# Second attention of a four-layer kernel: a pair's output product is issued before a head's products and transposed banks on TensorE

## What is computed

```python
q = jnp.einsum('qdh,bcd->bhcq', Q, x) * sq
k = jnp.einsum('qdh,bcd->bhcq', K, x) * sq
v = jnp.einsum('vdh,bcd->bhcv', V, x) * sv
att = jnp.einsum('bhcq,bhCq->bhcC', q, k) / d_query
att = jnp.where(causal, att, -jnp.inf)
p = jax.nn.softmax(att, axis=-1)
y = jnp.einsum('bhcC,bhCv->bhcv', p, v)
z = jnp.einsum('dvh,bhcv->bcd', W, y) * (math.sqrt(d_embed / d_value) / num_heads)
```

## Time and profile before

| | |
|---|---|
| median of 3 runs | 1491.33 us (1491.08 to 1492.69) |
| the profiled execution | 1491.82 us, span 1490.1 us |
| PE, busy of the span | 1212.1 us (81%) |
| DVE | 1099.0 us (74%) |
| ACT | 946.7 us (64%) |
| POOL | 757.9 us (51%) |

### The profile page before, as it was taken

One profiled execution on the slowest core, in us unless ns is written; L12 is line 12 of the kernel. 1 busy time (PEld: TensorE's weight loads), 2 busy tenths in 40 slices (PEclk: granted clock), 3 DMA queues, 4 the chain that ended last, 5 costly groups with the idle time before them and its releaser, 6 DMA issues. The chain is left out here.

```text
span 1490.1 us, 28115 instructions
## 1 busy us (share of the span) xinstructions
PE 1212.1 (81%) x7865; PEld 1037.6 (70%) x7865; DVE 1099.0 (74%) x2826; ACT 946.7 (64%) x2522; POOL 757.9 (51%) x950
## 2 busy tenths in 40 slices
PE   1587734999928898988998999999999997299992
PEld 1476633999817777777777777777777776199992
DVE  5666534777727788888888888888888886277774
ACT  1554421444418788888888888889898886154440
POOL 3004463444405555576575576675765765334443
PEclk9986656999959999999999999999999998599996
DMA  9391011222125656555555556565555652122215
GB/s 182 102 379 61 29 38 45 62 60 61 40 71 128 142 128 140 130 133 139 125 129 136 127 136 141 131 153 128 135 135 127 139 131 47 31 63 60 61 52 175
DMA packets 122658, 165.15 MB, mean 111 GB/s; under 512 B 40164, under 2 KB 84079, under 8 KB 122512
## 3 DMA queue, kind: packets, MB, share of 16 engines
q1 hardware_dynamic: 109648, 144.34, 41.1%
q0 software_dynamic: 8640, 16.93, 3.6%
q10 hardware_dynamic: 4224, 2.10, 0.5%
HBM read 26.59 MB, written 36.96 MB: 43 GB/s over the span
## 5 line engine op out<-in xcount | busy, mean ns | idle before, releaser
L1389 POOL TENSOR_TENSOR b_probs<-b_probs,b_recip 128x128 f32<-128x128 f32 (+3 forms) x512 | 352.1, 717 | 294.8 <-DVE b_recip L1622 294.8
L420 DVE TENSOR_TENSOR b_pt_lo<-b_ring,b_pt_hi 128x512 fp32r<-128x512 f32 (+1 forms) x384 | 229.7, 598 | 104.1 <-ACT b_pt_hi L414 101.7
L545 ACT ACTIVATE b_probs<-b_s_bank,b_neg_max 128x256 f32<-128x256 f32 (+3 forms) x512 | 266.2, 530 | 47.9 <-DVE b_neg_max L537 47.9
L1227 POOL DMA_INDIRECT y_rows<-f_y_sb,f_dest x142 | 138.8, 978 | 193.0 <-DVE f_y_sb L1200 185.2
L537 DVE TENSOR_REDUCE b_neg_max<-b_s_bank 128x1 f32<-128x256 f32 (+3 forms) x512 | 219.2, 479 | 11.1 <-PE b_s_bank L529 10.9
L1437 PE MATMUL b_s_bank<-b_stack 128*128 128x256 f32 (+3 forms) x1024 | 208.0, 338 | 13.8 <-DMA b_stack<-b_qk 7.5
L414 ACT ACTIVATE b_pt_hi<-b_ring 128x512 fp32r<-128x512 f32 (+1 forms) x384 | 204.8, 534 | 14.4 <-PE b_ring L485 11.3
L485 PE MATMUL b_ring<-ident,b_probs 128*128 128x128 f32 x1280 | 190.4, 281 | 13.3 <-DVE b_qk L420 12.6
L554 PE MATMUL b_pv_bank<-b_pt_hi,b_v 128*128 128x512 f32 (+3 forms) x512 | 161.4, 327 | 45.8 <-DVE b_pt_lo L420 45.5
L1170 ACT ACTIVATE f_hid_hi<-f_hid_bank 128x384 fp32r<-128x384 f32 x142 | 69.8, 491 | 160.1 <-PE f_hid_bank L1123 135.3
L485 PEld LDWEIGHTS b_ring<-ident,b_probs 128*128 128x128 f32 x1280 | 140.6, 141 | 41.6 <-DVE b_qk L420 21.1
(11 more groups left out here) (298 smaller groups left out, 3024.2 us busy)
## 6 DMA issues: line engine op xcount, KB each, us to landing
b_stack<-b_qk SPq DMA_DIRECT2D x128, 384.0 KB, 5.0
b_stack<-b_qk SPq DMA_DIRECT2D x128, 256.0 KB, 4.8
x_sorted<-a_blank SPq DMA_DIRECT2D x64, 260.0 KB, 3.5
b_stack<-b_qk SPq DMA_DIRECT2D x128, 128.0 KB, 4.9
f_xs<-x_sorted SPq DMA_DIRECT2D x142, 65.0 KB
b_yc<-y_rows SPq DMA_DIRECT2D x16, 256.0 KB, 4.2
f_yc<-y_rows SPq DMA_DIRECT2D x16, 256.0 KB, 5.1
y_rows<-f_y_sb,f_dest POOLq DMA_INDIRECT x142
```

Of the source, the lines that this page charges most:

```text
L420: nc.vector.tensor_tensor(dst, src(rg.of(key)), hi.bitcast(F32), ALU.subtract).then_inc(rg.lo_done, 1)
L545: nc.scalar.activation(probs[:, P_AT[i]:P_AT[i] + (i + 1) * P], s_tile(sc, i), ACT.Exp, bias=sc.neg_max[:, i:i + 1], accum_out=sums[:, i:i ...
L1227: nc.gpsimd.indirect_dma_start(out=g.y_rows, out_offset=bass.IndirectOffsetOnAxis(dest[:, i:i + 1], 0), in_=y_sb[i % NY][:], in_offset=Non ...
L1389: nc.gpsimd.tensor_tensor(part, part, recip[:, i:i + 1].to_broadcast([P, (i + 1) * P]), ALU.mult).then_inc(probs_done, 1)
```

## The change

In TensorE's program the output of a finished pair is issued before `products(u - 2)`; it stood between the first and the second transposed bank of head `u - 1`. Nothing else is touched: the waits of each step stay with it.

```diff
@@ -1481,14 +1481,13 @@
                     route_score(nc, pe, g, rt, rg, leaving(u, SCORED))
                 if leaving(u, COUNTED) is not None:
                     route_count(nc, pe, g, rt, rg, leaving(u, COUNTED))
+                if pair_behind(u, 5) is not None:
+                    output(pair_behind(u, 5))
                 if alive(u - 2):
                     products(u - 2)
                 if alive(u - 1):
                     pe.wait_ge(probs_done, u * QT)
                     head_transpose(nc, pe, rg, turns(u - 1), probs[(u - 1) % 2], 0, g.ident)
-                if pair_behind(u, 5) is not None:
-                    output(pair_behind(u, 5))
-                if alive(u - 1):
                     head_transpose(nc, pe, rg, turns(u - 1), probs[(u - 1) % 2], 1, g.ident)
                     head_transpose(nc, pe, rg, turns(u - 1), probs[(u - 1) % 2], 2, g.ident)
```

## The result

The changed kernel takes 1515.74 us (median of 4 runs, 1513.32 to 1516.68) against 1491.2 us before (median of 4 runs too); the ratio is 1.0162, 95% interval 1.0144 to 1.018. It is 24.5 us slower.

The account below looks back on a forecast made before the run. No engine alone was taken as the bound, but two chains side by side: TensorE's order, and ACT with DVE. Terms 2.4 + 0 + 17.6 + 8.4 = 28.4 us on 1491.82 gave 1520.2, for the median 1519.7 us; range 1507 to 1530.

Parts of the forecast that it names:

- (b): First pair of a sequence, 7 times: products and bank 0 queue behind output's x_done wait; 2.51 us each, 17.6 us slower.
- (c): TensorE idles 3.25 us before output in first-pair slots, its clock mostly falls to half; 1.2 us each, 8.4 us slower.
- (a): Ordinary odd slots: output fills TensorE's low-half wait, short waits delay bank 0; 2.4 us slower, TensorE's lead gains 0.
- TensorE's order is the bound: Second attention: each covered TensorE wait becomes gain, 34.6 us, so 17 us faster after first-pair losses, 1474 us; chance 0.06.
- Later waits absorb: After first-pair slots, ACT's waits for stack copies absorb delay, leaving about 1 us each; 1498 us; chance 0.07.
- The clock holds: TensorE's clock does not fall in first-pair slots, only ordinary-slot and queueing losses remain, 20.0 us; 1511.3 us; chance 0.22.
- The clock stays down: After first-pair waits TensorE's half clock lasts into the next slot, 2.7 us each, 18.9 us; 1530 us; chance 0.07.

Follow-up runs that it names:

- first pairs alone: Against the kernel before, only outputs of each sequence's first pair (u mod 16 = 5) moved in front of the products; 1518.68 against 1492.58 us, ratio 1.0184.
- the wait filled: Changed kernel plus eight spare matmuls before the wait for x_done in the 7 slots that wait; 1512.4 us, ratio 1.0131 to the kernel before.

## Why the prediction was right

The forecast was 1519.7 us in a range of 1507 to 1530; 1515.74 was measured. Step by step:

- *(b) The queue behind x_done.* 2.51 us for each of 7, 17.6 in all. Measured: 2.43 in the slot whose clock held, 2.42 (first slot) with first pairs alone, 2.39 to 2.45 with the wait filled, so 17.0. The half of it is right too: 1.19 for output and bank 0 alone, 1.17 measured. The waits for x_tok came to 21.8 us where 22 to 24 were named. ACT's new wait was 3.35 us at full clock (3.5 named). Undone alone, the kernel is back at 1.000; done alone, it costs 1.0184.
- *(c) The clock.* 8.4 us, taken as 1.2 for each of 7. The profiled execution has 25.5 - 17.0 = 8.5: six slots with 1.2 to 1.5 us over 2.43, one with none. That the sum fits so well is partly luck: 1.2 was a choice near the middle of wide bounds, two of 14 stretches of 2.7 us and more had no fall, and one fall cost between 0.5 us (1.70 less 1.17) and 2.1 us (4.53 less 2.42) in its slot. The Trainium skill, page TensorE: Matmul & The Clock Gate, section "Why this matters for your kernels", says that idle gaps between bursts of matmuls drop the array to half clock. Six of the seven slots agree. A gap by itself does not decide it here: the clock held after 3.31 us and fell after 1.90.
- *(a) Ordinary slots.* This term was mis-sized: 2.4 us, measured -0.5 (and 1.000 when done alone). The losses that I counted slot by slot came smaller: slot 11 lost 0.2 us where I had up to 0.45; of the two for which I had up to 0.36, slot 1 lost 0.13 to 0.2 in five of its eight and slot 9 nothing. Slot 13's 0.2 to 0.35 us are not its own output's but 11's and 12's, handed on: ACT's wait for the values rose from 7.6 to 10.7 us. And the gains, which I had set at 0, are larger: slots 12, 4 and 0 are 0.2 to 0.3 us shorter, 4.9 in all. ACT's wait for q, down from 4.6 to 2.2 us, is a part of it; the rest I have not traced. The reason given for why more is not gained fits: TensorE's lead ends at the low halves of q and k, a wait that rose by 10.9 us (12.2 to 23.1). No run shortens that wait by itself. The terms together are 25.0 us for 28.4, and most of the difference is this one.
- *Rivals.* "TensorE's order is the bound" asked for a gain in ordinary pairs and there was none. "Later waits absorb" fails for the change (slots 6 to 8 gave back nothing of the 25.5 us, they grew by 0.5) but it is what happened to the gain when output was moved behind bank 2: half of that came back in the next slot, mostly as waits for the copies. "The clock holds" is the kernel with the filled wait. "The clock stays down" fails as well: in the changed kernel it was at 1.00 again 3 to 4.5 us after each restart.

## What to carry to other kernels

Before moving a step forward in an engine's order, list its waits in its rarest case, not in the common one. Here 56 of 64 outputs cost nothing net, and 7 that wait for another engine's release cost 1.6%. The price is what is queued behind the wait, up to the instruction for which the next engine stands, and it can be added up from rows; when the release was made earlier, or the waiting step put behind what others need, the loss was gone. Filling an engine's wait can be worth nothing: 29 us of TensorE's waits were filled here for 0.0%. That this is so because a second chain of the same length, through ACT and DVE, runs beside it is argued from the waits, and no run shortens that chain alone.

## What the runs showed of the hardware

In the first-pair slots a fall of TensorE's clock cost 0.5 to 2.1 us in the slot, and whether it falls can't be told from the length of the idle stretch alone. It held at 1.00 after 2.70 us (seventh slot of the changed kernel) and after 3.31 us (first slot with first pairs alone), and it fell to 0.50 after 3.00 us (where it was still at 0.50 in 1208 to 1212, the first 4 us) and once after 1.90 us, while two other stretches of 1.90 us in the same kernel left it up. Eight spare matmuls, 2.03 us of work in a stretch of 3.3 us, kept it up in all seven slots.
